# Routed slots for the feed forwards of a three-stage transformer block

## The reference

```python
x = x + attn_a(layernorm(x))   # 8 heads of 128, relative positions, softmax over 1024 keys
x = x + ffn(layernorm(x))
x = x + attn_b(layernorm(x))   # 16 heads of 8, causal, one key and value head for all
x = x + ffn(layernorm(x))

def ffn(x):                    # E = 8 experts, H = 256
    scores = softmax(x @ Wg.T)
    val, idx = top_k(scores, 2)
    val = val / (val.sum() + 1e-9)
    comb = (one_hot(idx, E) * val[..., None]).sum(-2)
    out = 0
    for e in range(E):
        a, b = split(x @ W1[e].T + b1[e], 2)
        out = out + ((a * sigmoid(b)) @ Wo + bo) * comb[..., e:e+1]
    return out
```

## Time and profile before

| | us |
|---|---|
| median of 3 runs | 2802.12 (2799.71 to 2806.91) |
| the profiled execution | 2800.01 |
| its span, first to last instruction | 2798.3 |

### The profile page before, as it was taken

How to read it: one execution, slowest core, us unless ns; L and a number is a source line. 1 busy time by engine, 2 the same in 40 slices (tenths; PEclk the granted TensorE clock), 3 DMA queues, 4 the chain that set the end, 5 groups by cost and what they waited for, 6 DMA issues and landing times.

```text
span 2798.3 us, 45154 instructions
## 1 busy us (share of the span) xinstructions
PE 2620.7 (94%) x14496; PEld 2042.4 (73%) x14496; DVE 2037.5 (73%) x5225; ACT 1656.8 (59%) x3430; POOL 385.7 (14%) x813
## 2 busy tenths in 40 slices
PE   4999999999999999999999889989998989988998
PEld 3788788888888888888888667755555555545776
DVE  4677766767767777677776678878777777773887
ACT  3566666666666666665666445536666656655454
POOL 1000000000000000000110233402222212222344
PEclk8999999999999999999999989969999999998999
DMA  3665566566665666656666000000000000000000
GB/s 125 226 220 200 181 224 210 192 211 208 210 211 198 210 211 209 209 206 210 226 233 209 10 1 1 1 1 1 1 1 1 1 1 1 1 1 1 9 9 16
DMA packets 97587, 321.63 MB, mean 115 GB/s; under 512 B 11924, under 2 KB 25620, under 8 KB 97140
## 3 DMA queue, kind: packets, MB, share of 16 engines
q1 hardware_dynamic: 92650, 312.84, 32.6%
q0 software_dynamic: 1584, 4.33, 0.5%
q10 hardware_dynamic: 3120, 1.57, 0.2%
HBM read 158.53 MB, written 157.29 MB: 113 GB/s over the span
## 4 chain that ended last, share of the span: by engine, by line
PE 80%; DVE 11%; ACT 5%; issue 3%; POOL 1%; DMA 0%; SPq 0%; DVEq 0%; ACTq 0%; POOLq 0%
PE ps L243 8%; PE ps L245 7%; PE ps L244 7%; PE ps L630 7%; PE ps L743 5%; PE ps L605 5%; PE ps L604 5%; PE ps L781 5%; PE ps L643 4%; PE ps L645 4%; PE ps L644 4%; PE ps L763 4%; PE ps L675 4%; PE ps L676 4%; PE ps L677 4%
## 5 line engine op out<-in xcount | busy, mean ns | idle before, releaser
L910 ACT ACTIVATE a_Ph<-ps 128x512 fp32r<-128x512 f32 x512 | 305.9, 597 | 467.8 <-PE ps L630 467.7
L1215 DVE CUSTOM_DVE_ANT_0 a_sp<-ps,a_sp 128x1024 f32<-128x1024 f32 x256 | 313.2, 1223 | 180.0 <-PE ps L245 175.9
L980 ACT ACTIVATE r_P<-ps 128x512 f32<-128x512 f32 (+3 forms) x768 | 327.9, 491 | 187.1 <-PE ps L763 182.8
L1221 DVE TENSOR_TENSOR a_Pl<-ps,a_Ph 128x512 fp32r<-128x512 f32 x512 | 349.2, 682 | 10.0 <-ACT a_Ph L910 9.8
L604 PE MATMUL ps<-a_fa,a_ua 128*128 128x384 f32 (+2 forms) x960 | 327.2, 353 | 19.3 <-DVE a_fb L1176 13.9
L931 ACT ACTIVATE r_y<-ps 128x256 f32<-128x256 f32 x512 | 194.6, 385 | 216.6 <-PE ps L677 212.4
L903 ACT ACTIVATE a_sp<-a_sp,a_nm 128x1024 f32<-128x1024 f32 x256 | 295.0, 1152 | 32.1 <-DVE a_nm L1215 31.4
L630 PE MATMUL ps<-ident,a_sp 128*128 128x128 f32 x2048 | 309.0, 273 | 0.0
L743 PE MATMUL ps<-r_K,r_Q 128*128 128x512 f32 (+3 forms) x768 | 282.5, 403 | 18.2 <-DVE r_mx L1366 12.8
L630 PEld LDWEIGHTS ps<-ident,a_sp 128*128 128x128 f32 x2048 | 250.8, 141 | 61.7 <-issue 0.6
L605 PE MATMUL ps<-a_fb,a_ub 86*128 86x384 f32 (+2 forms) x960 | 290.8, 318 | 0.0
(11 more groups left out here) (217 smaller groups left out, 5676.0 us busy)
## 6 DMA issues: line engine op xcount, KB each, us to landing
scr<-a_rt SPq DMA_DIRECT2D x256, 576.0 KB, 3.1
a_sp<-scr SPq DMA_DIRECT2D x256, 512.0 KB, 4.4
a_wc<-wsp SPq DMA_DIRECT2D x24, 512.0 KB, 5.5
wsp<-a_wc SPq DMA_DIRECT2D x8, 512.0 KB, 5.6
a_ub<-a_ua SPq DMA_DIRECT2D x64, 44.0 KB
a_w1st<-in_w1t POOLq DMA_DIRECT2D x8, 256.0 KB, 4.6
out<-x SPq DMA_DIRECT2D x4, 512.0 KB, 3.2
a_w1r<-in_w1r POOLq DMA_DIRECT2D x8, 254.0 KB, 4.4
```

Source lines behind the costliest of these rows:

```text
L910: e.activation(self.Ph[:, n % 3, :], ps[:, 4 + n % 2, :], ACT.Copy).then_inc(S["p_hi"], 1)
L980: e.activation(self.P[:, pt, off:512], ps[:, bank, off:512], ACT.Exp).then_inc(S["b_exp"], 1)
L1215: e.tensor_tensor_reduce(out=w, in0=ps[:, 2:4, :].rearrange("p a n -> p (a n)"), in1=w, scale=-1.0, scalar=3e38, op0=ALU.add, op1=ALU.min, ...
L1221: e.tensor_tensor(self.Pl[:, n % 3, :], ps[:, 4 + n % 2, :], self.Ph[:, n % 3, :].bitcast(F32), ALU.subtract).then_inc(S["p_lo"], 1)
```

## The change

The feed forward of seven of the eight (layer, batch) pairs is done by routed slots; the last one (second feed forward, batch 3) stays with the dense form. For one routed batch (`routed(r)`):

- `m_rank`: one product with an upper triangle of ones and eight with all ones give for every row its rank within each expert and the experts' counts. `m_slot`: from the counts the number of 128-slot tiles per expert, the first slot of each expert, the expert of each of NS = 23 tiles (`mapi`), and for every row the two slots that its two experts give it (`slot`).
- `m_disp`: VectorE normalises a tile of `x` again, and GpSimd scatters its 128 rows to the two slots each (two indirect DMAs into DRAM, 512 B a row).
- `m_load`, `m_turn`, `m_mm`: SyncE loads four slot tiles at a time, TensorE transposes them, ScalarE and VectorE split them. TensorE loads the 23 expert numbers into registers once, and each slot tile is multiplied by the weights of the expert that its register names. ScalarE takes `tanh(b/2)` and VectorE `(tanh + 1) * a`, twice the gated value; `m_store` writes it to DRAM.
- `m_gath`, `m_sum`, `m_fin`, `m_proj`: GpSimd gathers a tile's 128 rows from their two slots (two indirect DMAs, 1 KB a row, into the one buffer `gb`), VectorE adds them by their weights (halved), and transposition, split, `Wo` and residual follow as before.

These units have no stage of their own. Three batches run inside the first attention, from step 64 b + 17 on, one step for each list in `routed`; four run inside the second, a part in each of its rounds. `plan_f` has eight tiles, with batch 3's normalisation and gates in front, and its gate is now two VectorE operations. `b_prepare` stands at the head of `plan_b`. The normalised rows are kept for two batches, not four; weights are loaded and split earlier (from step 52), and all eight low parts have a place of their own. Some semaphores are joined.

The core of the diff:

```diff
+NS = 2 * L // 128 + E - 1
+NG = (NS + 3) // 4
+NR = 7
...
+def routed(r):
+
+    place = [[("m_rank", r)], [("m_slot", r)]] + [[("m_disp", r, n), ("m_disp", r, n + 1)] for n in range(0, 8, 2)]
+    experts = []
+    for t in range(NS):
+        if t % 4 == 0:
+            experts.append([("m_turn", r, t // 4, 7)] + ([("m_load", r, t // 4 + 1)] if t // 4 + 1 < NG else []))
+        experts.append([("m_mm", r, t, 7)] + ([("m_store", r, t - 1)] if t else []))
+    back = [[("m_store", r, NS - 1)], [("m_gath", r, 0)], []]
+    for n in range(8):
+        back.append([("m_sum", r, n)] + ([("m_gath", r, n + 1)] if n < 7 else []) + [("m_fin", r, n, 7)])
+        back.append([("m_proj", r, n, 7)])
+    return place, experts, back
...
+        place, experts, back = routed(b - 1)
+        for i, its in enumerate(place + [[]] * 4 + [[("m_load", b - 1, 0)], []] + experts + back):
+            extra.setdefault(64 * b + 17 + i, []).extend(its)
...
+    p = splits(3)(B - 1, 7) + gates(1, B - 1)
...
+    out = [("b_prepare",)] + first(0) + spread(prepare(0) + chain(0), splits(1)(B - 1, 7))
+    late, tail = [("xb_bias", 0)], []
...
+        r = B - 1 + b
+        place, experts, back = routed(r)
+        half = len(experts) // 2
+        if g == 0:
+            late += (splits(3)(b - 1, 7) + gates(1, b - 1) if b else gates(0, B - 1)) + flat(place)
+        elif g == 1:
+            late += (splits(2)(b + 1, 7) + [("xb_bias", b + 1)] if b + 1 < B else []) + [("m_load", r, 0)] + flat(experts[:half])
+        elif g == 2:
+            late += flat(experts[half:] + back[:1])
+        else:
+            late += flat(back[1:])
...
+            rows = self.xsd[r % 2][512 * g:512 * g + 128 * k, :].rearrange("(k p) d -> p k d", p=128)
+            e.dma_start(self.sx[:, 0:k, :], rows).then_inc(S["d_xs"], 16)
+        else:
+            _, r, t = u
+            e.wait_ge(S["m_gate"], NS * r + t + 1)
+            if r >= 2 and t == 0:
+                e.wait_ge(S["m_sum"], 8 * (r - 1))
+            e.dma_start(self.gsd[r % 2][128 * t:128 * t + 128, :], self.gg[:, t % 3, :]).then_inc(self.d_gs[t % 3], 16)
...
+    def gpsimd_routed(self, e, u):
+        S = self.S
+        _, r, n = u
+        if u[0] == "m_disp":
+            e.wait_ge(S["m_xd"], 8 * r + n + 1)
+            if r == 0 and n == 0:
+                e.wait_ge(S["d_zero"], 48)
+            if r >= 2 and n == 0:
+                e.wait_ge(S["m_tr"], NG * (r - 1))
+            for k in range(2):
+                e.indirect_dma_start(self.xsd[r % 2], bass.IndirectOffsetOnAxis(self.slot[:, k, n:n + 1], 0),
+                                     self.xd[:, n % 2, :], None).then_inc(self.d_scat[n % 2], 16)
+        else:
+            if n == 0:
+                for t in range(NS - 3, NS):
+                    e.wait_ge(self.d_gs[t % 3], self.stored(r, t))
+            if 8 * r + n:
+                e.wait_ge(S["m_sum"], 8 * r + n)
+            for k in range(2):
+                e.indirect_dma_start(self.gb[:, k, :], None, self.gsd[r % 2],
+                                     bass.IndirectOffsetOnAxis(self.slot[:, k, n:n + 1], 0)).then_inc(S["d_gath"], 16)
...
+            e.matmul(ps[:, 7, 0:72], self.upper[:, :], self.both[:, :, :].rearrange("p n e -> p (n e)"), start=True, stop=False)
+            for n in range(8):
+                i = e.matmul(ps[:, 7, 8 * n + 8:72], self.ones[:, :], over(self.both[:, n, :], (0, 8 - n), (1, E)),
+                             start=False, stop=n == 7)
+            i.then_inc(S["m_rmm"], 1)
...
+            if t == 0:
+                e.wait_ge(S["m_map"], r + 1)
+                e.load(self.expert, self.mapi[0:1, 0:NS])
+                if r == 0:
+                    e.wait_ge(S["w1_lo"], E)
+            if t % 4 == 0:
+                e.wait_ge(S["m_xlo"], NG * r + t // 4 + 1)
+            e.wait_ge(*free[bank])
+            k, cs, hb = e.snap(self.expert[t], min_val=0, max_val=E - 1), slice(128 * (t % 4), 128 * (t % 4) + 128), ps[:, bank, :]
+            wh, wl = (w[:, bass.ds(k, 1), :].rearrange("p k n -> p (k n)") for w in (self.Wh, self.Wl))
+            e.matmul(hb, self.sxh[:, cs], wh, start=True, stop=False)
+            e.matmul(hb, self.sxh[:, cs], wl, start=False, stop=False)
+            e.matmul(hb, self.sxl[:, cs], wh, start=False, stop=True).then_inc(S["m_mm"], 1)
+            free[bank] = S["m_gate"], NS * r + t + 1
...
+            e.wait_ge(S["m_sum"], 8 * r + n + 1)
+            e.wait_ge(*free[bank])
...
+            e.activation(self.sig2[:, t % 2, :], ps[:, bank, FH:512], ACT.Tanh, scale=0.5).then_inc(S["m_sig"], 1)
...
+            many = tmp[:, 0:64].rearrange("p (e j) -> p e j", j=E)
+            self.step(e.tensor_tensor(many, over(self.rk[:, 64:72], (1, E), (0, E)), over(self.j128[:, :], (0, E), (1, E)), ALU.is_gt))
+            e.wait_ge(S["dve_step"], self.steps)
+            self.step(e.reduce_sum(self.tiles[:, :], many, axis=AX))
+            e.wait_ge(S["dve_step"], self.steps)
+            upto = tmp[:, 64:128].rearrange("p (e j) -> p e j", j=E)
+            self.step(e.tensor_tensor(upto, over(self.tiles[:, :], (0, E), (1, E)), le[:, :, :], ALU.mult))
+            e.wait_ge(S["dve_step"], self.steps)
+            self.step(e.reduce_sum(self.ends[:, :], upto, axis=AX))
...
+        elif u[0] == "m_disp":
+            n = u[2]
+            i = 8 * r + n
+            if i >= 2:
+                e.wait_ge(self.d_scat[n % 2], 32 * (i // 2))
+            e.tensor_scalar(self.xd[:, n % 2, 0:127], x[:, 8 * b + n, 0:127], self.mv[:, 1, n, 0:1], self.rs[:, 1, n:n + 1],
+                            ALU.subtract, ALU.mult).then_inc(S["m_xd"], 1)
...
+            e.scalar_tensor_tensor(self.gg[:, t % 3, :], self.sig2[:, t % 2, :], 1.0, ps[:, bank, 0:FH], ALU.add,
+                                   ALU.mult).then_inc(S["m_gate"], 1)
...
+        elif u[0] == "m_sum":
+            n = u[2]
+            e.wait_ge(S["d_gath"], 32 * (8 * r + n + 1))
+            if 8 * r + n:
+                e.wait_ge(S["m_ftr"], 8 * r + n)
+            self.step(e.tensor_scalar(self.sacc[:, :], self.gb[:, 0, :], self.pw[:, r % 2, n, 0:1], None, ALU.mult))
+            e.wait_ge(S["dve_step"], self.steps)
+            e.scalar_tensor_tensor(self.sacc[:, :], self.gb[:, 1, :], self.pw[:, r % 2, n, 1:2], self.sacc[:, :], ALU.mult,
+                                   ALU.add).then_inc(S["m_sum"], 1)
...
+            self.step(e.scalar_tensor_tensor(xs, self.fbo[:, :], self.csum[:, 8 * b + n:8 * b + n + 1], xs, ALU.mult, ALU.add))
+            e.wait_ge(S["dve_step"], self.steps)
+            e.wait_ge(S["m_pmm"], 8 * r + n + 1)
+            e.tensor_tensor(xs, ps[:, bank, 0:128], xs, ALU.add).then_inc(S["m_out"], 1)
...
-                e.scalar_tensor_tensor(dst, ps[:, i % 4, 0:FH], self.comb[:, n, k:k + 1], self.sig[:, i % 4, :],
-                                       ALU.mult, ALU.mult).then_inc(S["f_gate"], 1)
+                e.wait_ge(S["f_sig"], i + 1)
+
+                self.step(e.scalar_tensor_tensor(self.sig[:, i % 4, :], self.sig[:, i % 4, :], 1.0, ps[:, i % 4, 0:FH],
+                                                 ALU.add, ALU.mult))
+                e.wait_ge(S["dve_step"], self.steps)
+                e.tensor_scalar(dst, self.sig[:, i % 4, :], self.comb[:, n, k:k + 1], None, ALU.mult).then_inc(S["f_gate"], 1)
...
```

More of the change, by code:

```diff
@@ L11 @@
 U32 = mybir.dt.uint32
+I32 = mybir.dt.int32
 ACT = mybir.ActivationFunctionType
@@ L134, in plan_a, with plan_f @@
             p += [("tlow", pq, jb), ("pv", pq, ja)]
[L135 to L143 removed]
+        p += extra.pop(s, [])
+    return p + [u for s in sorted(extra) for u in extra[s]]
+def plan_f():
+    p = splits(3)(B - 1, 7) + gates(1, B - 1)
+    for n in range(8):
         for k in range(E):
[L145 removed]
+            p.append(("f", n, k))
             if n and k == 1:
[L147 removed]
+                p.append(("f_merge", n - 1))
             if n and k == 3:
[L149 removed]
+                p.append(("f_fin", n - 1))
             if n and k == 6:
[L151 to L156 removed]
+                p.append(("f_proj", n - 1))
+    return p + [("f_merge", 7), ("f_fin", 7), ("f_proj", 7)]
 def spread(many, few, start=0):
@@ L210, in finish @@
         return r, prev, price
-    out = first(0) + prepare(0) + chain(0)
-    late, tail = splits(2)(B - 1, 7) + [("xb_bias", b) for b in range(B)], []
+    flat = lambda steps: [u for its in steps for u in its]
+    out = [("b_prepare",)] + first(0) + spread(prepare(0) + chain(0), splits(1)(B - 1, 7))
+    late, tail = [("xb_bias", 0)], []
     for n in range(16):
@@ L227, in plan_b @@
             late += [(u, b, half) for half in range(2) for u in ("b_out", "b_out2")]
-        if g == 0 and b:
-            late += splits(3)(b - 1, 7) + gates(1, b - 1)
         total, goal, done, spent = sum(price), sum(cost(u) for u in side), 0, 0
@@ new lines, in memory @@
+        self.sth, self.stl = sb("th", [128, FH], F32R), sb("tl", [128, FH], F32R)
+        self.xd = sb("xd", [128, 2, 128])
```

(30 more changed lines are left out.)

598 lines of the change are left out of this document (363 added, 235 removed).

## The result

The changed kernel takes 2957.39 us (median of 4 runs, 2957.15 to 2959.20) against 2803.30 for the kernel before beside it: ratio 1.0551, 95% interval 1.0533 to 1.0569. It is slower by 5.5%; the forecast was 2710.

The account below looks back on a forecast made before the run. TensorE was taken as the fullest engine in all four stretches, with VectorE room only in the attentions. Stages of 1710 + 892 + 105 = 2707 us, plus 1.7, gave 2709, forecast as 2710; 8-in-10 range 2600 to 2880.

Parts of the forecast that it names:

- The second attention: Stage with four routed batches: 730 + 104 + 16 + 25 + 17 = 892 us.
- I take 200: Second attention, per batch: VectorE 177 and TensorE about 178 us, with today's idle share, make 200; four batches add 104.
- The sign that was named: Second attention: VectorE over 85% busy, idle before the weighted sums only for half a microsecond.
- The first attention: Stage with three routed batches, tail and preparation: 1564 + 81 + 31 + 6 + 3 + 20 + 5 = 1710 us.
- 31 + 6 + 3: First attention: 31 us TensorE waiting for weighted sums, 6 slot arithmetic delaying scores, 3 register loads.
- The sum's picture of the outgoing transposes: First attention: TensorE waits 1.3 us for the weighted sum before each of 24 outgoing transposes, 31 us.
- the last stage: Last batch's dense feed forward, alone at the end: 105 us, VectorE the fullest engine, normalisation and gating exposed for 25.
- rival (c): ScalarE: Tanh not served where Exp is, so table loads add at least 200 us, 2910 or above; chance 0.03.
- rival (a): Both attentions: side work fits the gaps, the second goes up by 80 us in all, total 2620; chance 0.18.
- (b): GpSimd's indirect issues decide and the kernel is slower than before; 2858 us at 2 us an issue; chance 0.22.
- the break-even: GpSimd: at 1.66 us per indirect issue the 92 us of gain are gone.
- (d): Expert matmuls: register-indexed operands expose 0.4 us per pair, 64 us in all, total 2774; chance 0.09.

Follow-up runs that it names:

- e12: Kernel without routed work, plus the routed work of TensorE, VectorE and ScalarE from constants, without handshakes or transfers: 2714.89 us.
- e18: Changed kernel with both the indirect scatters and the indirect gathers left out: 2856.82 us.
- e5_peonly: Kernel without routed work, plus TensorE's routed matmuls and transposes from constants, with no waits and no other engine's routed work: 2670.78 us.
- e1: Changed kernel with expert weights chosen by a constant in place of a register, and no registers loaded: 2956.97 us.
- e22_stages2: Changed kernel with only dispatch in the attentions, scatters spread, experts and sums mostly in own stages, more banks and buffers: 2763.85 us, ratio to before 0.9857.

## Why the prediction was wrong

**The second attention (892, measured 1068) is the step that failed.** Its three layers: 730 to 899 is work (normalisations and gates 29, the routed work of all engines 140), which the term "I take 200" per batch had at 104. 899 to 980 is handshakes, 81 us, for which the sum had no term: it counted waits only where GpSimd brings one. 980 to 1068 is transfers, 88 us, where it had 58 (gathers 43 against 16, scatters 45 against 25; the masks' part of these, 38, against 17). The 200 came from busy sums of two engines plus an idle share taken as fixed. e12 against e18 shows that it isn't: the same work takes 81 us more once each piece has to pass through three engines. The sign that was named failed with it: VectorE was to be over 85% busy there, and is 63% (668 of 1068).

**The first attention (1710 with tail and preparation, measured 1792).** Normalisations and gates that came into it: 16, not in the sum. TensorE's work 108 against 81. The price of the matmuls was right: in e5_peonly, from each start to the next, they take 84 us before the mark, the rank product 1 us per batch where 2 was taken. The other 24 us fall on the attention's own instructions around them: the work doesn't lengthen this attention one for one, but more, and why no run tells. VectorE's and ScalarE's beside it 10. Handshakes 51 and indirect transfers 8 against 31 + 6 + 3 = 40. The sum's picture of the outgoing transposes was right (TensorE's list there has 19 waits for the weighted sum, 24.4 us, 1.3 each), but moving them gave 14 us, not 31. Tail 38 against 25.

**Right:** the last stage (97.5 against 105; its start to the first expert product 17 against 25, the rest 81 against 80), with VectorE its fullest engine; the indirect issue (0.97 + 0.30 against 1.1); registers, taken at 1 us per batch, where e1 shows none, though the gaps that were to be a sign of being wrong are in the trace (91 us); and Tanh: in the changed kernel no table load stands at its line 1029. By that the Trainium skill's page ScalarE: Activation LUTs (Table sets) agrees, and rival (c) didn't happen. Gathers landed in 2.8 us, between the 3.3 taken and 2.3, the estimate by the Trainium skill's page DMA: Bandwidth & Descriptors (Anatomy of one DMA). Two slips in its sums change nothing of this: the last batch's terms add up to 9.0 us a tile, not 9.2, and rival (a), with 80 us in place of 162, should have taken off 82, not 60.

**The rivals.** (a) was on the other side: the pieces found no gaps. (b) had the side of the result and a wrong mechanism: GpSimd's price stayed below the break-even, and without any indirect transfer the kernel still takes 2857. (d) had an idle time that is in the trace and costs nothing. Missing was a rival by which pieces in an attention cost 73 us per batch against 66 and 60 in a stage, wherever the wait falls.

## What to carry to other kernels

Before work is moved from a stage of its own into gaps of another, ask how many engines each piece passes through: where the host stage consists of short turns between two engines, a piece costs its work, plus a wait at every hand-over, plus what stands behind it in each queue. Price this by building the new work up in layers (none, one engine from constants, all engines, hand-overs, transfers); idle time in a list of waits is no price, as attempts on the three largest ones here gave 0 us or lost 7 and 94. And keep a queue that the critical engine depends on (here masks on GpSimd) free of bursts: more buffers left the burst as long as it was; spreading the scatters over more of the attention, in e22_stages2, broke it.

## What the hardware showed that was not expected

VectorE stood still under a GpSimd fill. Timeline of the changed kernel at the start of the second attention's preparation:

```profile
1777.55 6.92 POOL L579 MEMSET r_K<- 128x8192 f32 x1
1778.42 6.19 DVE L1399 TENSOR_SCALAR m_acc<-m_gb,m_pw 128x256 f32<-128x256 f32 x1 [0.94 <-DMA m_gb<-gsd,m_slot]
1784.65 0.48 DVE L1401 SCALAR_TENSOR_TENSOR m_acc<-m_gb,m_pw,m_acc 128x256 f32<-128x256 f32 x1
```

The first product of a weighted sum, 0.45 us in the mean of 56, took 6.19 and ended with the fill (1784.61 against 1784.47). Not every VectorE instruction stands still so: in the kernel before, the same fill (1567.9 to 1574.8 us) ran beside gates and additions of VectorE (lines 1270 and 1276) at their usual 0.48 and 0.42 us. The Trainium skill's page SBUF — State Buffer (SBUF: two separate sides) says that the two engines share one port pair, which goes for a whole instruction to whichever starts first, and that only certain forms of VectorE instruction need it; both traces agree, though no run here tests the form. e22_stages2 cuts this fill into pieces on ScalarE.
